# First attention layer of a two-layer kernel: scores three heads ahead, values split in bulk, low parts and product moves on other engines

## The reference

```python
q = _split_heads(hidden_states @ Wq.T, H)
out_text = _merge_heads(_attend(q, k, v, sm_scale))        # 77 keys
out_ip = _merge_heads(_attend(q, k_ip, v_ip, sm_scale))    # 435 keys
out = (out_text + IP_SCALE * out_ip) @ Wo.T + bo + residual
```

## Time and profile before

| | us |
|---|---|
| median of 3 runs | 1819.99 (1816.65 to 1820.86) |
| the profiled execution's own time | 1818.08 |
| its span | 1816.3 |
| heads of layer 0, batches 0 to 3 | 121.1, 120.6, 121.3, 120.0 |
| heads of layer 1, with the tail, batch 0 | 265.5 |
| TensorE's mean granted clock | 0.958 of full |

### The profile page before, as it was taken

How to read it: one execution, slowest core, us unless ns; L and a number is a source line. 1 busy time by engine, 2 the same in 40 slices (tenths; PEclk the granted TensorE clock), 3 DMA queues, 4 the chain that set the end, 5 groups by cost and what they waited for, 6 DMA issues and landing times.

```text
span 1816.3 us, 34149 instructions
## 1 busy us (share of the span) xinstructions
PE 1648.9 (91%) x8640; PEld 1240.3 (68%) x8640; DVE 1279.8 (70%) x3564; ACT 1116.6 (61%) x2323; POOL 462.0 (25%) x1225
## 2 busy tenths in 40 slices
PE   5788999999888889999988889999998889999993
PEld 2454479999445448999835545999974554799991
DVE  2587268887678627888758853888875883588875
ACT  1598157775279626777429943777734991577760
POOL 0244013232034202323104411223201440232320
PEclk9899989999989998999989998999998999899996
DMA  7210210000301031000031111100012102000000
GB/s 233 75 35 22 89 63 22 17 20 3 120 25 37 10 105 53 21 17 17 1 121 33 37 45 62 60 18 19 12 55 74 37 23 87 27 21 18 18 5 15
DMA packets 44947, 80.39 MB, mean 44 GB/s; under 512 B 4145, under 2 KB 9521, under 8 KB 44849
## 3 DMA queue, kind: packets, MB, share of 16 engines
q1 hardware_dynamic: 40736, 71.52, 11.9%
q10 hardware_dynamic: 4112, 7.73, 1.4%
HBM read 45.16 MB, written 34.08 MB: 44 GB/s over the span
## 4 chain that ended last, share of the span: by engine, by line
PE 78%; ACT 9%; issue 5%; DVE 5%; DMA 1%; ACTq 1%; POOL 1%; SPq 0%; POOLq 0%; DVEq 0%
PE ps_w L836 38%; PE ps_s L836 17%; PE ps_t L836 16%; PE ps_b L836 4%; ACT probsT_high L454 4%; ACT probsT L462 3%; DVE row_max L639 2%; PE ps_m L836 2%; ACT q_slot L447 1%; POOL probsT_low L376 0%; ACT probs L471 0%; ACT probs L529 0%; DMA w_ki<-in_wki 0%; PE ps_b L942 0%; DVE probs L805 0%
## 5 line engine op out<-in xcount | busy, mean ns | idle before, releaser
L454 ACT ACTIVATE probsT_high<-ps_t 128x512 fp32r<-128x512 f32 x640 | 382.6, 598 | 121.7 <-PE ps_t L836 117.4
L628 DVE TENSOR_TENSOR probsT_low<-probsT,probsT_high 128x512 fp32r<-128x512 f32 x560 | 393.1, 703 | 79.1 <-ACT probsT L462 69.8
L836 PE MATMUL ps_w<-gram,probsT_high 128*128 128x416 f32 (+2 forms) x1280 | 388.9, 315 | 0.0
L462 ACT ACTIVATE probsT<-ps_t 128x512 f32<-128x512 f32 x640 | 384.2, 600 | 0.0
L836 PE MATMUL ps_w<-gram_low,probsT_high 128*128 128x384 f32 (+2 forms) x1280 | 352.6, 304 | 0.0
L488 ACT ACTIVATE probs<-ps_s,exp_bias 128x508 f32<-128x508 f32 x320 | 220.4, 689 | 126.4 <-POOL exp_bias L387 82.4
L836 PE MATMUL ps_t<-q_slot,k_slot 98*128 98x512 f32 x640 | 267.4, 436 | 10.1 <-ACT q_slot L447 9.4
L836 PE MATMUL ps_s<-k_slot,q_slot 96*128 96x512 f32 x640 | 248.3, 432 | 27.3 <-issue 12.1
L387 POOL TENSOR_SCALAR exp_bias<-row_max 128x1 f32<-128x1 f32 x320 | 129.1, 403 | 560.5 <-DVE row_max L670 560.5
L836 PEld LDWEIGHTS ps_w<-gram_low,probsT_high 128*128 128x128 f32 (+1 forms) x1280 | 243.4, 190 | 11.0
L836 PEld LDWEIGHTS ps_w<-gram,probsT_high 128*128 128x128 f32 (+1 forms) x1280 | 242.0, 189 | 11.4
(11 more groups left out here) (156 smaller groups left out, 2093.4 us busy)
## 6 DMA issues: line engine op xcount, KB each, us to landing
q_slot<-parts_q SPq DMA_DIRECT2D x160, 96.0 KB
k_slot<-parts_k SPq DMA_DIRECT2D x160, 96.0 KB
parts_k<-probsT_high SPq DMA_DIRECT2D x24, 512.0 KB, 4.3
parts_q<-probsT_low SPq DMA_DIRECT2D x24, 512.0 KB, 4.3
parts_k<-probsT_high SPq DMA_DIRECT2D x24, 128.0 KB, 3.8
parts_q<-probsT_low SPq DMA_DIRECT2D x24, 128.0 KB, 3.5
ctx_sb<-in_ctxT ACTq DMA_DIRECT2D x3, 1024.0 KB, 8.2
outT<-x_sb ACTq DMA_DIRECT2D x8, 256.0 KB, 4.9
```

What stands on the lines that cost most here:

```text
L454: nc.scalar.activation(probsT_high[1 - par][:, t, :], ps_t[:, t % 2, :], ACT.Exp, scale=SCALE)
L462: nc.scalar.activation(probsT[:, t, :], ps_t[:, t % 2, :], ACT.Exp, scale=SCALE).then_inc(pt_block[l], 1)
L628: nc.vector.tensor_tensor(probsT_low[1 - par][:, t, :], probsT[:, t, :], probsT_high[1 - par][:, t, :].bitcast(F32), ALU.subtract).then_in ...
L836: return nc.tensor.matmul(out, lhsT, rhs, start=start, stop=stop)
```

## The change

- **Row maxima.** A new `run_heads0` gives layer 0 a fourth role: in a step of head n, TensorE makes the first and the second half of the scores of head n+3; VectorE takes the second half's maxima one step later, ahead of all else, and the row of maxima goes to ScalarE (`shifted`) between its exps 1 and 2, where it lay between 2 and 3. There is one more step ahead of the heads of a batch. The first block of transposed scores is made a step earlier than before; the others and the values' matmuls change places.
- **Low parts.** GpSimd subtracts for blocks 1, 2 and 3 of a head, VectorE for block 0 alone.
- **Product.** VectorE moves `ps_w` (68x512) to SBUF, ScalarE no longer does.
- **Values.** ScalarE rounds the values of all heads (5 instructions of up to 128x320 a batch), VectorE forms all low parts (`v0_lows`, 5 instructions), in the tail behind its last products and ahead of its last addition; the ring's banks of the value jobs are now credited to VectorE. A slot is filled by two copies on GpSimd, one step ahead and not two.
- Small buffers move inside larger ones, and the identity is the rounded one.

```diff
@@ -43,8 +43,12 @@
 STORES = 2 * 3 * 16
 
 
-V0W = 2 * (D + 1)
+V0H = D + 1
+V0W = 2 * V0H
 V0S = 2 * V0W
+AHEAD = 3
+LOWS_DVE = 1
+LOWS_POOL = TB - LOWS_DVE
 
...
@@ -63,8 +67,8 @@
 NEXT = (
     [("k0", m, "D") for m in range(CBN)]
     + [("q0", m, "D") for m in range(CBN)]
-    + [("v0t", 0, "A")]
-    + [("v0i", t, "A") for t in range(TB)]
+    + [("v0t", 0, "D")]
+    + [("v0i", t, "D") for t in range(TB)]
...
@@ -267,6 +275,20 @@
             for k in range(SLOTS):
                 step(b, HEADS - SLOTS + k, k, TURNS - 1, True, k < SLOTS - 1, k < SLOTS - 2)
 
+        def run_heads0(step, eng, b):
+
+
+
+            step(b, -3, 1, -1, False, False, False, True)
+            step(b, -2, 2, -1, False, False, True, True)
+            step(b, -1, 3, -1, False, True, True, True)
+            with eng.Fori(0, TURNS - 1) as turn:
+                for k in range(SLOTS):
+                    step(b, SLOTS * turn + k, k, turn, True, True, True, True)
+            for k in range(SLOTS):
+                n = HEADS - SLOTS + k
+                step(b, n, k, TURNS - 1, True, n + 1 < HEADS, n + 2 < HEADS, n + AHEAD < HEADS)
+
         def load_ctx(eng, batch):
             eng.dma_start(ctx_sb[:, :, :], ctxT[batch, :, :].rearrange("(k p) t -> p k t", p=P)).then_inc(ctx_in, 16)
...
-            def step0(b, n, k, turn, use, transposed, scores):
+            def step0(b, n, k, turn, use, transposed, shifted, scores):
                 par = k % 2
-                if scores:
-
-                    pool.wait_ge(oT_moved, HEADS * b + n + 1 + CREDIT) if use else None
+                g = HEADS * b + n
+                def low(t):
+
+                    pool.wait_ge(pt_block[0], TB * (g + 1) + t + 1 + CREDIT1)
                     pool.sem_inc(passed, 1)
...
+                    nc.gpsimd.tensor_tensor(probsT_low[1 - par][:, t, :], probsT[:, t, :],
+                                            probsT_high[1 - par][:, t, :].bitcast(F32), ALU.subtract).then_inc(low_pool, 1)
+
+                if transposed:
+                    for t in range(LOWS_DVE, TB - 1):
+                        low(t)
+
+                    pool.wait_ge(oT_moved, g + CREDIT)
                     pool.sem_inc(passed, 1)
...
+                    by_part = v0_slot[1 - par][:, :, :].rearrange("p t (g w) -> p t g w", w=V0H)
+                    nc.gpsimd.tensor_copy(by_part[:, :, 0:2, 0:D], v0_ip[:, :, n + 1, :, :])
+                    nc.gpsimd.tensor_copy(by_part[:, 0, 2:4, 0:D], v0_text[:, n + 1, :, :]).then_inc(v0_in, 1)
+                    low(TB - 1)
...
-                elif t < TB - 1:
-                    act.wait_ge(low_block[0], (TB - 1) * g + t + 1 + CREDIT)
+                elif t < LOWS_DVE:
+                    act.wait_ge(low_block[0], LOWS_DVE * g + t + 1 + CREDIT)
                 else:
-                    act.wait_ge(low_last, g + 1 + CREDIT)
+                    act.wait_ge(low_pool, LOWS_POOL * g + t - LOWS_DVE + 1 + CREDIT)
...
-            def step0(b, n, k, turn, use, transposed, scores):
+            def step0(b, n, k, turn, use, transposed, shifted, scores):
                 par = k % 2
                 if transposed:
                     expT(b, 0, n, par, 0)
                     expT(b, 0, n, par, 1)
-                if use:
-                    act.wait_ge(oT_done, HEADS * b + n + 1)
-                    nc.scalar.activation(outT0[par], ps_w[par][0:V0S, :], ACT.Copy).then_inc(oT_moved, 1)
+                if shifted:
+                    shift(b, 0, n + 1, k + 1)
                 if transposed:
                     expT(b, 0, n, par, 2)
-                if scores:
-                    shift(b, 0, n + 1, k + 1)
                 if transposed:
                     expT(b, 0, n, par, 3)
...
+            def v0_high(b):
+
+                def by_head(name, t):
+                    wait_job(act, b, name, t)
+                    return bank(name, t)[:, 0:C].rearrange("p (h d) -> p h d", d=D)
+
+                nc.scalar.activation(v0_text[0:TEXT0, :, 1, :], by_head("v0t", 0)[0:TEXT0, :, :], ACT.Copy).then_inc(v0_high_in, 1)
+                for t in range(TB):
+                    nc.scalar.activation(v0_ip[:, t, :, 1, :], by_head("v0i", t),
+                                         ACT.Copy, scale=ip_rows[:, :] if t == 0 else 1.0).then_inc(v0_high_in, 1)
...
+            def v0_lows(b):
+
+                before = 0 if b is FIRST else (1 + TB) * (b + 1)
+
+                def by_head(name, t, k):
+                    wait_job(dve, b, name, t)
+                    dve.wait_ge(v0_high_in, before + k + 1)
+                    return bank(name, t)[:, 0:C].rearrange("p (h d) -> p h d", d=D)
+
+                nc.vector.tensor_tensor(v0_text[0:TEXT0, :, 0, :], by_head("v0t", 0, 0)[0:TEXT0, :, :],
+                                        v0_text[0:TEXT0, :, 1, :].bitcast(F32), ALU.subtract).then_inc(freed["D"], 1)
+                for t in range(TB):
+                    nc.vector.scalar_tensor_tensor(out=v0_ip[:, t, :, 0, :], in0=by_head("v0i", t, 1 + t),
+                                                   scalar=ip_rows[:, 0:1] if t == 0 else 1.0,
+                                                   in1=v0_ip[:, t, :, 1, :].bitcast(F32),
+                                                   op0=ALU.mult, op1=ALU.subtract).then_inc(freed["D"], 1)
...
-            def step0(b, n, k, turn, use, transposed, scores):
+            def step0(b, n, k, turn, use, transposed, shifted, scores):
-
-                def maxima(half):
+                g = HEADS * b + n
+
+                def maxima(j, rows, half):
 
                     cs = slice(2 * half, 2 * half + 2)
-                    dve.wait_ge(s_half, 2 * (HEADS * b + n + 2) + half + 1)
+                    dve.wait_ge(s_half, 2 * j + half + 1)
+                    nc.vector.tensor_reduce(out=rows[:, cs, 0:1], in_=ps_s[:, :, 0:TEXT0], axis=AX.X, op=ALU.max)
...
-                if scores:
-                    maxima(0)
+                if shifted:
+                    maxima(g + 2, row_max[0][par], 1)
                 if transposed:
                     lowT(b, 0, n, par, 0)
                 if scores:
-                    maxima(1)
-                if transposed:
-                    lowT(b, 0, n, par, 1)
+                    maxima(g + AHEAD, row_max[0][1 - par], 0)
                 if use:
-
-                    dve.wait_ge(o_done, HEADS * b + n + 1)
-                    nc.vector.tensor_reduce(out=o0_all[:, n, :, :],
-                                            in_=ps_b[:, 0:SC * V0S].rearrange("p (c a w) -> p c w a", c=SC, a=2),
+                    dve.wait_ge(oT_done, g + 1)
+                    nc.vector.tensor_copy(outT0[par], ps_w[par][0:V0S, :]).then_inc(oT_moved, 1)
+                if use:
+
+                    dve.wait_ge(o_done, g + 1)
...
+                                            in_=ps_b[:, 0:SC * V0S].rearrange("p (c v a w) -> p c v w a", c=SC, v=2, a=2),
                                             axis=AX.X, op=ALU.add).then_inc(o_moved, 1)
-                if transposed:
-                    lowT(b, 0, n, par, 2)
...
@@ -807,6 +833,8 @@
                     if ahead and i < 2:
                         for m in ((0,), (1, 2))[i]:
                             low(b, "q0", m)
+                    if ahead and i == 3:
+                        v0_lows(b)
                     link(b, last)
...
@@ -822,6 +850,7 @@
 
             lows(FIRST, "k0")
             lows(FIRST, "q0")
+            v0_lows(FIRST)
             run_batches(dve, batch)
...
-                    pe.wait_ge(max_half, 2 * (g + 2) + half + CREDIT)
+                        pe.wait_ge(slots_in[0][(k + AHEAD) % SLOTS], SLOT_LOADS * (TURNS * b + turn + (k + AHEAD) // SLOTS + 1))
+                    pe.wait_ge(max_half, 2 * (g + AHEAD) + half + CREDIT)
                     for i in range(2):
-                        last = scores_chunk((k + 2) % SLOTS, 2 * half + i, ps_s[:, i, :])
+                        last = scores_chunk((k + AHEAD) % SLOTS, 2 * half + i, ps_s[:, i, :])
...
                 def values_low(t):
-                    if t < TB - 1:
-                        pe.wait_ge(low_block[0], (TB - 1) * g + t + 1 + CREDIT)
+                    if t < LOWS_DVE:
+                        pe.wait_ge(low_block[0], LOWS_DVE * g + t + 1 + CREDIT)
                     else:
-                        pe.wait_ge(low_last, g + 1 + CREDIT)
+                        pe.wait_ge(low_pool, LOWS_POOL * g + t - LOWS_DVE + 1 + CREDIT)
                     return mm(ps_w[par][0:V0S, :], v0_slot[par][:, t, :], probsT_low[par][:, t, :], False, t == TB - 1)
 
+                if transposed:
+                    scoresT_of(0, g, k, 1)
+                if use:
+                    pe.wait_ge(oT_moved, g - 1 + CREDIT)
+                    pe.wait_ge(v0_in, g + 1)
+                    for t in range(TB):
+                        values_high(t)
+                if transposed:
+                    scoresT_of(0, g, k, 2)
+                if shifted:
```

(32 more changed lines are left out.)

104 lines of the change are left out of this document (39 added, 65 removed).

## The result

The changed kernel takes **1831.31 us** in the median of 4 runs (1829.25 to 1833.51), beside 1818.32 for the kernel before on the same chip (4 runs, 1815.7 to 1820.86): a ratio of **1.0071** (95% interval 1.0053 to 1.009), so 0.7% slower. The forecast was 1826, range 1803 to 1846. The profiled execution took 1830.29 with a span of 1828.4, 12.1 more than the span of before.

A forecast was written before the change was run, and what follows sets the result against it. With no engine full in layer 0's heads, a closed chain of waits was taken as the bound. Heads -4 and tails +10 made +6 on the profiled 1818.08, 1824; that execution lay 1.9 below the median, so 1826 us, range 1803 to 1846.

The forecast's parts named there:

- The heads: Layer 0's heads: faster pace, longer beginning, low clock and shorter end give -1.0 us a batch, -4 us in four.
- The pace: Time per head in layer 0: 5.30 us against 5.49 before, -3.4 us a batch over 18 heads.
- Chain G: Closed chain in the heads: block 2's exps, GpSimd low part, copies, high products, row of maxima, shift; 5.28 us a head.
- Chain V: Closed chain of VectorE and TensorE in the heads: both halves' maxima, scores, transposes, addition; 5.20 us a head.
- The beginning: Start of each batch's heads: one more scores half before the first product, +2.4 us, and +0.3 for the low clock.
- The end of the heads: End of each batch's heads: loses about 0.3 us less than a full head, counted as -0.3 a batch.
- The tail: Low parts and a later fourth value job ahead of the last addition delay the transposes 3.3 us; three tails +10 us.
- Slots' loads: Loads into the slots ahead of the heads: some 5.2 us against about 7.5 until the scores, so hidden, no cost.
- Rival 1: Tail hidden but for 0.6 us of the later fourth job: -4 in heads, +2 in tails, 1818 us; chance 0.15.
- Rival 2: ScalarE becomes the bound in the heads: pace 4.95 us, total 1798 us; chance 0.15.
- Rival 3: Shared port in the heads: VectorE's low part waits up to 0.6 us for GpSimd's, pace 5.8, 1863 at worst; chance 0.15.
- Rival 4: Row of maxima in the heads comes no earlier, pace stays 5.49 us, total 1840 us; chance 0.15.

The follow-up runs named there:

- e4_no_inc: Changed kernel without the semaphore increment between the wait and the subtraction of GpSimd's low parts: 1835.02 us, ratio to the kernel before 1.0082.
- e2_copies_first: Changed kernel with GpSimd's two slot copies ahead of its three low parts: 1835.11 us, ratio to the kernel before 1.0077.
- e1_tail: Changed kernel with one low part of the values ahead of the tail's last products and four behind its last addition: 1824.38 us, ratio to before 1.0027.
- e10_shares: Changed kernel with slot copies first, both halves' maxima in one step, four value low parts behind the tail's addition, old engine shares: 1800.95 us, ratio to before 0.9911.
- e3_two_lows: Changed kernel with VectorE forming two low parts a head and GpSimd two: 1924.74 us, ratio to the kernel before 1.056.
- e9_order: Changed kernel with the old shares: ScalarE moves the product, VectorE forms three low parts, GpSimd one: 1935.32 us, ratio to the kernel before 1.0633.
- e7_both: Changed kernel with slot copies ahead of GpSimd's low parts and both halves' maxima in one step on VectorE: 1801.97 us, ratio to before 0.9917.

## Why the prediction was right, point by point

- **The time** (1826 forecast, 1831 measured) and its sign came out, the time by luck in good part. The heads were forecast at -4 and measured +12.25, so this term had the wrong sign: per batch the pace brought -0.76 and not -3.4, the beginning cost +4.1 and not +2.7. The tails were forecast at +10; measured are +10.6 in the tails themselves and +3.0 behind them. These terms alone would make +26. Layer 1, the last batch and the start, for which the sum had no term, gave 13.8 back.
- **The pace** (5.30 forecast, 5.44 measured) is the term that was mis-sized. The chains were the right two: opening each alone did nearly nothing, opening both brought 0.5 us a head. Chain G, 5.28 forecast, is 5.43, and it was short by two hand-overs. From block 2's exps to GpSimd the prediction had 0.08, measured 0.18, an increment standing between wait and subtraction (without it, in e4_no_inc, the pace falls to V's). From the copies to the high products it had 0.05, measured 0.25. Against these stand 0.06 each on the low part and the first copy, which follow more closely than their durations. Chain V, 5.20 forecast, was 5.35 in e2_copies_first: 0.57 and not 0.46 from a scores half that waited to the block behind it, 0.71 and not 0.67 to the maxima.
- **The beginning** (+2.7 forecast, +4.1 measured in the mean of four batches): the first product comes 16.38 after the first scores (57.77 to 74.15), before it was 12.16. The half of the scores in front, head 2's second (72.28), was right at 2.55 us, from 69.73. Two things were missing. Two transposed blocks stand between it and the first product (0.85, from 73.30 to 74.15), and another one ahead of them, at 68.72, waits 0.75 for ScalarE with the row of head 1's maxima right behind it, so that it is 6.38 from head 1's first half of the scores to head 2's where it was 5.55. All of this is at the lower clock.
- **The end of the heads**: -0.3 forecast, -0.27 measured in the mean; the four batches have -0.02, -0.77, -0.71 and +0.40, so this agreement is chance.
- **The tail** (3.3 forecast, 3.5 measured). With the products ending 0.40 later, the fourth job began at 483.19 and not 482.85, the rounding at 485.65, the low part at 486.12, the addition at 486.52: the chain is the one written down, but for the 0.24 us from the addition's end to the transposes. What the forecast left out as "up to 2 us each" came in two of three: 1.4 and 1.6.
- **Slots' loads** were hidden, as said: from 85 to 165 us no wait of TensorE ends on a DMA.
- **The signs.** From 85 to 165 us GpSimd is 82% busy and its copy releases the high products, and the tail's idle 2.63 us are there. Three signs of being right failed: the transposes of the product lie 5.44 us apart and not 5.2 to 5.4, the first product comes 4.2 us later and not 2 to 3, and ScalarE waits for the row of maxima (7.9 us in these 80) and not for transposed scores. No sign of being wrong came.
- **Rival 1** (tail hidden) fell: +3.5, and e1_tail gains 8 us by undoing it. **Rival 2** (ScalarE the bound) was not the changed kernel, whose ScalarE idles 0.51 for the row of maxima in the head shown; it is e10_shares. **Rival 3** (the port) fell for the change, at 0.682 for VectorE's low part, and shows in e3_two_lows, beside the clock, and in e9_order. Where VectorE's 0.68 meets GpSimd's instruction it becomes up to 1.58, where GpSimd's copy of 0.29 meets VectorE's it becomes 0.76: by the rule that the prediction took from the Trainium skill (SBUF — State Buffer, "SBUF: two separate sides"), the blocked engine waits for the other's whole instruction, and these rows agree. On who comes first one row does not: in e3_two_lows GpSimd's instruction starts at 117.42 and VectorE's at 117.86, yet GpSimd's is the one that is stretched, and it ends 1.13 behind the end of VectorE's (118.54 to 119.67). Why is not shown. VectorE's move out of PSUM at 117.22 lies beside GpSimd's low part at 117.37, which takes 1.28, and neither is stretched. **Rival 4** (the pace stays 5.49) was nearest to the measured pace, not to its cause: the row of maxima follows the block ahead of it without a gap, 114.82 to 115.06.

## What to carry to other kernels

Where no engine is full, list all closed chains with every hand-over in them, and cut all that lie within a tenth of each other: one at a time shows nothing, as here with 0.02 to 0.06 against 0.5 us. What moving work to an idle engine is worth hangs on the order, here 0.2 us a head in one and 1.5 in the other; put what that engine owes to TensorE (the copies) ahead of what is needed later (the low parts). Work formed in bulk must not stand ahead of the instruction that ends a stage: with one of the five instructions ahead of the last products and four behind the addition, the tail took 2.13 us where it had taken 2.02 before and 5.50 with all five in front. And read where a small gain goes: 7 us won in one stage did not show in the time, and the granted clock of the others had fallen.

## What the runs showed of the hardware

- A GpSimd subtraction begins 0.08 us after the exp that it waits for the earlier trace rows, but 0.18 where a semaphore increment stands between wait and subtraction; a matmul that waits for a GpSimd copy begins 0.25 after that copy's end (119.03 to 119.28).
- In the tail TensorE's granted clock fell to the lower level around the transposes in 18 of the 24 tails with an idle stretch of 2.6 to 2.8 us ahead of them (over the 13 us from there 0.61 in e2_copies_first's first tail, 0.89 in the changed kernel's), and not with the same 2.63 us in e7_both's first tail (1.00), nor in any of the twelve tails without such a stretch. From the tail's addition to the next batch's first maxima the three named are 21.7, 19.1 and 17.6 us. So the price of such a gap is not one number, here between nothing and 4 us; when it is paid stays open.
- With the same work, the part behind the last batch's heads took 310.5 us in the kernels where the lower level was granted for 34 us of it and 315.5 in the one where it was granted for 45.
